# Fetching the last chunk's rows in every third iteration in place of every fourth

## The reference

```
msg  = einsum('ebo,eb->eo', einsum('ei,bio->ebo', x[src], weight), w_comp[etype]) * edge_weight[:, None]
x    = layernorm(x + relu(segment_sum(msg, dst) + bias))
norm = deg_inv[dst] * ew           # ew with a self loop of weight 1
x    = layernorm(x + segment_sum(norm[:, None] * (x @ W)[src], dst) + b)
```

## Time and profile before

| what | value |
|---|---|
| median of 3 runs | 3417.73 us (3417.02 to 3420.3) |
| the profiled execution | 3414.11 us, its span 3412.3 us |
| mean granted TensorE clock over it | 0.728 of full |
| PE busy | 2179.1 us (64%) |
| POOL busy | 1482.1 us (43%), 1548 of its instructions are the gathers of L723 |
| DVE, ACT busy | 1436.0 us (42%), 852.2 us (25%) |
| row fetches by SP | 1920 DMAs of 256 bytes |

### The profile page before, as it was taken

The page is one execution under the profiler, slowest core; times in us unless marked ns, Lnnn a source line. Parts: engine busy times, 40 slices in busy tenths (PEclk is TensorE's granted clock), DMA queues, the critical chain, the costliest instruction groups (busy, mean ns, idle before and its releaser), DMA issues.

```text
span 3412.3 us, 68688 instructions
## 1 busy us (share of the span) xinstructions
PE 2179.1 (64%) x23108; PEld 1546.6 (45%) x23108; DVE 1436.0 (42%) x4064; ACT 852.2 (25%) x2162; POOL 1482.1 (43%) x1574
## 2 busy tenths in 40 slices
PE   3665555566656656666666766667666667766687
PEld 2443334344444444444444544445444445544476
DVE  5554445344444344444343443333533334333334
ACT  3332223222222222222222222221222222222211
POOL 5545554454444444444444444444444444343420
PEclk8777776666677676777677677677777777777788
DMA  3332222222222323222223222222232222222266
GB/s 88 91 121 92 92 92 83 67 74 81 78 80 71 100 90 92 71 88 81 71 83 91 63 85 85 83 88 69 57 89 66 76 67 73 77 84 70 89 224 212
DMA packets 192467, 301.86 MB, mean 88 GB/s; under 512 B 68109, under 2 KB 124365, under 8 KB 185985
## 3 DMA queue, kind: packets, MB, share of 16 engines
q1 hardware_dynamic: 128794, 242.80, 21.1%
q0 software_dynamic: 49632, 50.92, 7.4%
q10 hardware_dynamic: 13703, 3.79, 0.5%
HBM read 188.04 MB, written 109.32 MB: 87 GB/s over the span
## 4 chain that ended last, share of the span: by engine, by line
PE 49%; another core or an unknown queue 22%; issue 18%; ACT 4%; DVE 4%; SPq 2%; DMA 1%; ACTq 1%; DVEq 0%
PE types_ps L1135 6%; PE node_ps L1135 6%; PE sums_ps L1135 5%; PE dense_ps L1135 5%; PE coefs_ps L1235 5%; PE coefs_ps L1202 5%; ACT room L941 3%; PE coefs_ps L1251 3%; PE sums_ps L1168 3%; PE sums_ps L1153 2%; PE coefs_ps L1121 1%; SPq L596 1%; DVE first_room L1698 1%; PE node_ps L1140 1%
## 5 line engine op out<-in xcount | busy, mean ns | idle before, releaser
L723 POOL DMA_INDIRECT gathered_rows<-in_x,idx x1548 | 1464.9, 946 | 1799.9 <-ACT idx L825 1387.0
L1722 DVE TENSOR_TENSOR dve_ps<-coefs_ps,edges 128x40 f32<-128x40 f32 x196 | 39.9, 204 | 1078.8 <-PE coefs_ps L1121 551.0
L941 ACT COPY room<-dense_ps 128x294 f32 x390 | 168.7, 433 | 1040.9 <-remote 392.2
L1135 PE MATMUL sums_ps<-first_room 128*128 128x294 bf16 (+1 forms) x1170 | 320.8, 365 | 162.0 <-issue 109.6
L1135 PE MATMUL dense_ps<-first_room 128*128 128x294 bf16 x1170 | 311.4, 350 | 147.0 <-ACT room L941 70.9
L1135 PE MATMUL types_ps<-first_room 128*128 128x294 bf16 x1170 | 319.9, 361 | 110.6 <-issue 70.8
L1135 PE MATMUL node_ps<-first_room 128*128 128x294 bf16 x1170 | 316.0, 358 | 101.1 <-issue 74.8
L1698 DVE TENSOR_TENSOR first_room<-first_room,dve_ps 128x1024 bf16<-128x1024 bf16 x585 | 364.6, 676 | 0.0
L1782 DVE TENSOR_TENSOR acc_room<-acc_room,sums_ps 128x88 f32 x196 | 47.6, 243 | 616.5 <-remote 335.2
L941 ACT COPY room<-node_ps 128x294 f32 x390 | 168.8, 433 | 455.3 <-remote 224.6
L1693 DVE TENSOR_TENSOR first_room<-dve_ps,first_room 128x2352 bf16<-128x2352 f16 (+1 forms) x195 | 280.5, 1438 | 0.0
(11 more groups left out here) (290 smaller groups left out, 3618.5 us busy)
## 6 DMA issues: line engine op xcount, KB each, us to landing
acc_room<-block_table SPq DMA_DIRECT2D x208, 374.5 KB
fetched_rows<-in_x SPq DMA_DIRECT2D x1920, 0.2 KB
block_table<-room SPq DMA_DIRECT2D x11, 2621.5 KB
type_rows<-in_edge_type SPq DMA_DIRECT2D x260, 96.0 KB
gathered_rows<-in_x,idx POOLq DMA_INDIRECT x1548
first_room<-block_table SPq DMA_DIRECT2D x61, 374.5 KB, 6.4
block_table<-room SPq DMA_DIRECT2D x9, 2247.0 KB
block_table<-room SPq DMA_DIRECT2D x9, 1872.5 KB
```

The source lines that it names most:

```text
L723: pool.indirect_dma_start(gathered_rows[:, s, j, 0:D], None, rows, bass.IndirectOffsetOnAxis(ap=idx[:, s, j:j + 1], axis=0)).then_inc(rows ...
L941: nc.scalar.copy(blocks_out[:, h % 2, :, bass.ds(offset, nodes)], dense_ps[j % 4][:, 0:nodes * TILES].rearrange("p (w h) -> p h w", h=TILE ...
L1135: last = nc.tensor.matmul(main, lo_hot[:, w, j // 2, :, j % 2], node_hot[:, j // 2, 0:values, j % 2], start=(j == 0 and w == 0), stop=(w = ...
```

## The change

Two constants. Rows are fetched for every third iteration (5, 8, ..., 62: 20 of them, before 15), in portions of 44, 42 and 42 over the three iterations that end in the fetched one. POOL's loop body becomes three iterations long, its loop runs 20 times, and after it come iterations 63 and 64.

```
-FETCHES = 4
+FETCHES = 3
 FETCHED = [i for i in range(FETCHES, ITERS) if i % FETCHES == FETCHES - 1]
-FETCHED_ROWS = (24, 40, 32, 32)
+FETCHED_ROWS = (44, 42, 42)
```

## The result

| | time, us |
|---|---|
| before, measured beside it | 3417.38 median (3411.26 to 3420.3, 4 runs) |
| after | 3465.20 median (3463.06 to 3474.04, 4 runs) |
| ratio after / before | 1.0152, 95% interval 1.0137 to 1.0166 |
| forecast | 3434 (3411 to 3456) |
| profiled execution after | 3463.06, its span 3461.2 |

The change made the kernel 48 us (1.5%) slower. The forecast had the sign, at +17 us; the time lies 9 us above its range and 5 us under rival C in full. Where did the time go? First the page after: busy time by engine, the chain that ended last, the gathers, and the row fetches among the DMA issues.

What follows compares the result with a forecast made beforehand. PE was taken to be held while POOL's gather groups are under way. Terms -6.0 + 12.9 + 4.3 + 2.0 + 3.5 = +16.7 us on a median of 3417.73 gave 3434, range 3411 to 3456.

Steps and rivals of the forecast that it cites:

- rival C: Iterations 22 to 31: PE waits in full for the first unit; 3470, or half of it 3452; chance 0.13.
- (a): POOL: five gathers fewer, 1.2 us gained for each, 6.0 us in all (bounds 4.5 and 6.9).
- (b): SP: 640 more DMAs lengthen third steps; +12.9 us (iterations 31 to 47), +4.3 (48 to 62), +2.0 (5 to 21).
- (c): One unit buffer, iterations 22 to 30: late fetches delay units; 0.5 us in seven iterations, +3.5 us (0 to 40).
- (d): The waits around the fetched rows that the change touches: nothing added, no cost.
- A: Rows are free and only the gathers count: 4.5 to 6.9 us faster, 3411 to 3413; chance 0.18.
- B: Rows cost about what the gathers give, 7.2 us against 6.0: 3419, no change to tell; chance 0.14.
- D: Shorter gather groups free PE in the next steps too, 2.5 us a gather, rows free: 3405; chance 0.07.

Runs made afterwards that it cites:

- c3_no_rows: The changed kernel with rows fetched only for the first fetched iteration, gathers unchanged: 2082.32 us, against 2379.54 for the kernel before.
- c4_no_rows: The kernel before with rows fetched only for the first fetched iteration, gathers unchanged: 2087.60 us against 2379.54 for the kernel before.
- e4_even: The kernel before with portions of 32, 32, 32, 32 rows in place of 24, 40, 32, 32: 3410.61 us against 3416.49.
- experiment 7: The changed kernel without the rows of four sets, no fetch in iterations 21 to 32: 3430.93 us against 3416.49 for the kernel before.
- m4_fetch_early: The kernel before with all but each set's first portion issued ahead of the second step's unit loads: 2154.46 us against 2379.32.
- before_again: The kernel before, with no edit, on a chip of the 2379 kind: 2378.47 us.
- p_all_pool: The kernel before with POOL gathering every chunk and SP fetching no rows: 2107.44 us against 2379.32.

## Why the prediction was wrong

**(a) Five gathers, -6.0 us: right as far as the runs tell.** c3_no_rows and c4_no_rows have it at -5.3, on the other kind of chip, where POOL is the limit once SP is out of the way. On the first chip the steps of after agree: the third steps of iterations 35 and 38, with 7 gathers, took 17.95 and 17.97 us, those of 34, 36 and 37 with 8 took 18.67, 19.38 and 19.38, so 1.2 us for a gather.

**(b) Rows in iterations 5 to 21 and 31 to 62, +19.2 us: the sum near by luck, the price wrong.** The price was 0.99 us for a portion of 40 rows over one of 24 or 32, the mean of three windows over five others. Third steps after, all with 42 or 44 rows, of iterations 33, 34, 45 and 46:

```profile
1634.51:1653.37 18.86, 7.57 (x8) 0.80 0.09 19
1684.66:1703.33 18.67, 7.58 (x8) 0.73 0.08 16
2261.41:2280.24 18.83, 7.57 (x8) 0.73 0.09 20
2314.60:2335.09 20.49, 7.57 (x8) 0.75 0.13 33
```

The forecast had 19.7 us for such steps. Iterations 33, 34, 36, 37, 45 and 46 have a mean of 19.27 us after, 19.19 before (three of them with 40 rows) and 19.50 in e4_even (32 rows in each). The number of rows doesn't order them. The long step of iteration 45 before (20.49) is found in iteration 46 after (20.49) and in e4_even (20.48, with 32 rows), so it wasn't the 40 rows that made it long. Five against three windows of one execution were too few for 0.99 us.

Where the one price stood almost by itself it failed: iterations 32 to 38, before and then after.

```profile
1512.96:1868.15 355.19, 227.90 (x2373) 160.16 (x2371) 141.94 (x379) 84.42 (x217) 157.72 (x167) 0.71 0.27 79
```
```profile
1552.86:1906.75 353.89, 227.48 (x2372) 160.14 (x2369) 142.18 (x381) 84.30 (x217) 156.12 (x166) 0.71 0.27 79
```

They are 1.3 us shorter, where five more long portions and two gathers fewer were to give +2.6. The 14.8 us of the stretch lie behind them. PE stands 5.1, 9.6, 3.3 and 2.2 us at the first unit in iterations 40 to 43, and the five iterations 39 to 43 take 267.98 us against 260.54, 7.4 more. In iteration 48 the first unit is issued 13.2 us after its first gather (2400.20), where before it was 0.4 us ahead of it (2341.58); that iteration takes 60.72 us against 55.57, 5.2 more. Both look like (c)'s mechanism, late units, which I had set at nothing after iteration 31; no run took these rows out. So 14.8 us for 12.6 is luck. The stretch of 5 to 21 has +8.1 for -0.4. There SP loads no units but one at the very end, and what it holds up was not tried. Iterations 3 and 4, set at nothing give or take half a microsecond, have +3.0 with those ahead of them.

**(c) The one-buffer stretch, +3.5 us: the step that failed most.** "Against a full price: iteration 26, with the wait, took 50.61 us, iteration 25 without it 49.43. So at most 1.2 us of 4.38 remained" took a single pair of iterations for a price per wait. Two things stood wrong in it. The price of a wait: the nine waits grew from 7.3 us (4.4, 1.5 and 1.4; the others too short to list) to 65.2, and the time of the stretch by 28.8, half of that growth, where the forecast had 0.5 us for a wait of 5.7 to 6.9, less than a tenth. The longer waits are no longer hidden as the one of 4.38 us nearly was. That was rival C's mechanism, between its half and its full price (some 21 and 40 us for the stretch), and experiment 7 takes it out: without the rows the waits go, and the time with them. And the waits were longer than reckoned: the six that don't follow a third portion came out as forecast (mean 5.8), but the row loads of L592 were taken at the price of before (0.63 us a row with all in it), while every third portion paid 6 us more for a start off the grid of four. The diff shows it, 44 + 42 = 86; the trace of before, with all starts on the grid, could not show the price.

**(d) No new wait for `fetched_rows`: right.** PE's matmul of the fetched chunk, and all that it waited for:

```profile
L1153 PE MATMUL sums_ps<-fetched_rows,chunk_factors x40: 219/311/314, 303.7 to 3235.9; 128*32 128x64 f32 x40
its engine sat idle before it (us, times) until:
  issue: 2.7, 3
```

Of the rivals, A, B and D fell: the kernel is 48 us slower, not faster or the same. The rule of the Trainium skill under A, "DMA: Bandwidth & Descriptors", section "Issuing engines are not separate DMA queues", is that starting DMAs from several engines saves only the sequencer's time of issue. The time of issue was just what counted here: SP's sequencer is the queue in which the units stand, and m4_fetch_early shows 225 us for the order in that queue alone, on the 2379 kind.

What stays open. How the 48 us on the 3417 kind divide between the loads and the 640 rows: SP's portions grew there by 476 us, 120 of them at the third portion's loads, and on the other kind the loads made 95 of 257 us; but no run took them apart there. Why PE's work shows late around each gather group there, and not on the other chips. What the rows hold up in iterations 5 to 21 on that kind, and whether late units make the loss after iteration 38.

## What to carry to other kernels

Before work is given to an engine that "only issues", look at what stands behind it in that engine's queue and which engine waits for that; a long sum of waits on it is no spare time at the place where the work is put. A wait that is hidden today sets no price for a longer one: find how long the cover is, and take the full price beyond it. And three windows against five are no price either, until a run that changes nothing else has shown it. When a cut is moved, look at the addresses it makes as well as the counts: a portion that starts at column 86 in place of 88 cost three times the load. Last, a kernel has another limit under the one that is lifted: with SP out of the way POOL's 1.25 us a gather set the time.

## What the runs showed of the hardware that was not expected

- A load of 16 numbers from a row of SBUF into SP's registers took 1.17 to 1.25 us from a column that is a multiple of four, and 3.47 to 3.58 us from any other that was tried (22, 23, 38, 39, 62, 63, 78, 79, 86, 94, 97, 102, 110); 8 numbers took 0.79 and 1.94 us (medians by column).
- The same program took 3417 us on chip 14 and on the chip of the first measurement (perhaps the same), and 2379 on five others, with waits that have no known releaser (422.0 us for ACT's copies of PE's sums alone) on the first and none for these copies on the second, and a 1.5% loss on the first was 10.9% on the second. On the first, semaphores went up a median of 2.1 us after the recorded end of L1153's last matmuls, on the second 0.04 us. A verdict found on one chip kept its sign here, and not its size.
- On the quicker kind, POOL issues an indirect gather of 128 rows every 1.25 us, and nothing else sets the time where SP is not late (505.59 us for 404 gathers in before_again, 963.81 for 768 in p_all_pool). Bringing 128 rows by single transfers of 256 bytes from SP in place of one such gather cost the kernel 18 us (270 for 15), and all of it after iteration 21, where unit loads stand behind them.
